# Weight columns for the v and q projections: one cast-on-the-way load per column on GpSimd's queue, or two f32 half loads on SP's queue with a VectorE cast behind each

## Chip, cores and metric

One Trainium2 chip, all 8 NeuronCores; each core runs the same program on its own 2048 tokens. The metric is the device time of the slowest core in microseconds.

## The reference, cut to what matters

A layer on x of shape (2, 8192, 2048): a retention-style attention, a layer norm over x plus its result, then a mixture of 8 experts (top 2) and a second layer norm.

```python
q = (x @ Wq.T).reshape(Bsz, Ls, NHEAD, HEAD_DIM)
v = (x @ Wv.T).reshape(Bsz, Ls, NHEAD, HEAD_DIM)
ret = _retention_scan(v, lam)          # state = lam * state + v_t, along the tokens
out = (q * ret).reshape(Bsz, Ls, D)
out = _layernorm(out, ln_gamma, ln_beta)
g = jax.nn.silu(x @ Wg.T)
out = out * g
return out @ Wo.T
```

and around it `x = _layernorm(x + attn(x))`, `x = _layernorm(x + ffn(x))`, where the feed-forward part is silu(x W1) * (x W3) times the routing weight, then W2, summed over the experts.

## The kernel before

Each core holds 2048 tokens, feature-major (a feature on a partition, tokens along the free dimension), and works on them in two halves of 1024 (`emit_half`, line 486), each in two chunks of 512 columns (CW). A prefix stage first sums the tokens before the core's own, weighted by powers of lambda (lines 357 to 378), so that the scan can start from a carry. All bf16 weights pass through one ring of four SBUF slots, `wring` (line 216), 128 x 2048 bf16 each. `load_wcol` (line 243) takes the next slot and issues a single DMA on GpSimd's queue that reads 1 MB of f32 from HBM and writes it as bf16. It waits only until the matmuls that read the slot four columns ago are done, so the loads run ahead of TensorE.

The stage around the change is the loop over the 16 heads (mt) in lines 517 to 616. Per head:

1. v group: 32 matmuls (16 contraction tiles by 2 chunks, line 525) with a column of Wv into PSUM banks 0 and 1; in half 0 also 16 matmuls of one column (line 537) that apply the same weights to the prefix sum.
2. ScalarE copies v to SBUF (line 552, two copies); VectorE copies the carry (line 561, half 0), scans v along the tokens (line 572) and saves the last state (line 583).
3. q group: 32 matmuls with a column of Wq into banks 2 and 3 (line 596).
4. VectorE multiplies q by the scan's result into yS (line 608, two products).

Every engine runs its instructions in program order. Order between engines is by semaphores alone: each step carries the tokens that it waits for (`Prog.step`, line 56), and a `Buf` collects who last wrote and who read a buffer. A step's place on its engine is the place in this Python code where it is recorded. `begin_write` returns the readers and the last writer that a new write must wait for:

```python
def begin_write(self):
    d = self.readers + ([self.ready] if self.ready else [])
    self.readers = []
    return d
```

Behind the loop come the sums for the layer norm (lines 634, 642), the gate projection (line 663, GpSimd loads again), the norm's rows (`ln_rows_bcast`, line 410) and its application (lines 691 to 705), the output projection (line 737) with its x tiles loaded by SP (line 724), the router, and, behind a barrier, the experts (lines 1012, 1030, 1105) and the last norm with the stores of the output on ScalarE's queue (lines 1194 to 1208). x for a half is loaded as 16 casting DMAs on GpSimd's queue (line 504). The second half's x and first weight columns can be loaded while the first half's tail still runs.

Of the kernel before, what the change touches and what calls it, by code (L numbers as in the profile page):

```python
# [18 lines left out]
F32 = mybir.dt.float32  # L19
# [6 lines left out]
P = 128  # L26
D = 2048
KT = D // P
# [11 lines left out]
class Prog:  # L40

    def __init__(self, nc):
        self.nc = nc
        self.sems = {}
        self.counts = {}
        self.steps = {e: [] for e in ENGINES}
        names = ["dS", "dN", "dX", "pe", "dve", "act", "pool", "sp"]
        names += [f"dG{i}" for i in range(4)] + [f"dR{i}" for i in range(4)]
        names += [f"dW{i}" for i in range(4)] + [f"dA{i}" for i in range(4)]
        names += [f"dC{i}" for i in range(4)]  # L50
        names += [f"out{i}" for i in range(4)]
        for s in names:
            self.sems[s] = nc.alloc_semaphore(s)
            self.counts[s] = 0
# [80 lines left out]
def build(TC=2048, PREF=6144, CW=512):  # L135
# [7 lines left out]
    nc = bass.Bass("TRN2", target_bir_lowering=False)  # L143
    pr = Prog(nc)
# [4 lines left out]
    wq_d = dt("wqT", [KT, P, KT, P], F32, kind="ExternalInput").ap()  # L149
    wv_d = dt("wvT", [KT, P, KT, P], F32, kind="ExternalInput").ap()  # L150
# [65 lines left out]
    wringS = [A(f"wring{i}", [P, KT * P], BF16) for i in range(NWR)]  # L216
# [10 lines left out]
    wring = Ring(NWR)  # L227
# [11 lines left out]
    gbufB = [[Buf() for _ in range(FT)] for _ in range(2)]  # L239
    xcR = Ring(2)  # L240
    ntbR = Ring(2)

    def load_wcol(src_ap):
        s, b = wring.next()
        X = int(np.prod(src_ap.shape[1:]))
        tok = pr.dma("pool",
                     lambda en, t=wringS[s], sr=src_ap, X=X: en.dma_start(  # L247
                         out=t[:, 0:X], in_=sr),
                     deps=b.begin_write(), sem=f"dG{s}")
        b.wrote(tok)  # L250
        return s, b, tok
# [21 lines left out]
        out=wgfS[:], in_=wgf_d.rearrange("p kt e -> p (kt e)")), sem="dX")  # L273
# [5 lines left out]
        out=identf[:], in0=identf[:], scalar1=0.0, scalar2=None,  # L279
# [8 lines left out]
        out=e8f[:], in0=e8f[:], scalar1=0.0, scalar2=None,  # L288
# [6 lines left out]
        out=t16[:], in0=hbetaS[:], scalar1=NEGLN2, scalar2=None,  # L295
        op0=ALU.mult), deps=[t_hbeta])
    t_l0 = pr.tick("act", lambda en: en.activation(
        out=t16[:], in_=t16[:], func=AF.Exp), deps=[t_lpre])
    t_l1 = pr.tick("dve", lambda en: en.tensor_scalar(
        out=lam16[:], in0=t16[:], scalar1=-1.0, scalar2=1.0,  # L300
        op0=ALU.mult, op1=ALU.add), deps=[t_l0])
    t_l2 = pr.tick("dve", lambda en: en.tensor_scalar(
        out=lam16[:], in0=lam16[:], scalar1=1.0, scalar2=TINY,
        op0=ALU.min, op1=ALU.max), deps=[t_l1])
    t_l3 = pr.tick("act", lambda en: en.activation(
        out=loglam16[:], in_=lam16[:], func=AF.Ln), deps=[t_l2])
# [25 lines left out]
    for kt in range(KT):  # L332
        dep = [t_wgf, t_ones_bf]
        if kt == 0:
            dep += psB[5].begin_write()
        wsum_grp = pr.step("pe", lambda en, kt=kt: en.matmul(
            out=psS[5][0:E, 0:1], lhsT=wgfS[:, kt * E:(kt + 1) * E],
            rhs=onescol_bf[:], start=(kt == 0), stop=(kt == KT - 1)),
            deps=dep, inc="pe" if kt == KT - 1 else None)
    psB[5].wrote(wsum_grp)  # L340
    t_wsum = pr.tick("dve", lambda en: en.tensor_copy(
        out=wsumC[:], in_=psS[5][0:E, 0:1]), deps=[wsum_grp])
# [3 lines left out]
    for h in range(NH):  # L346
        t = pr.tick("act", lambda en, h=h: en.activation(
            out=preW[:, h:h + (PT - 1) * NH + 1:NH], in_=cexpS[:],
            func=AF.Exp, scale=loglamP[:, h:h + 1]),
            deps=[t_cexp, t_loglamP])  # L350
        t_preW.append(t)
    t_preWb = pr.tick("dve", lambda en: en.tensor_copy(
        out=preWb[:], in_=preW[:]), deps=t_preW)
# [3 lines left out]
    for j in range(PT):  # L357
        slot, wb, tld = load_wcol(xpre_d[j * P:(j + 1) * P, :])
        last = None
        for c in range(ZCH):  # L360
            dep = [tld, t_preWb]
            if j == 0:
                dep += psB[c].begin_write()
            tok = pr.step("pe", lambda en, j=j, c=c, slot=slot: en.matmul(  # L364
                out=psS[c][0:NH, 0:512],
# [3 lines left out]
                deps=dep, inc="pe" if c == ZCH - 1 else None)  # L369
# [10 lines left out]
    for c in range(ZCH):  # L380
        t = pr.tick("dve", lambda en, c=c: en.tensor_copy(
            out=ZS[:, c * 512:(c + 1) * 512], in_=psS[c][0:NH, 0:512]),
            deps=[z_tok[ZCH - 1]])
# [3 lines left out]
    for kt in range(KT):  # L387
        d4 = psB[4].begin_write()
        tt_ = pr.tick("pe", lambda en, kt=kt: en.transpose(
            out=psS[4][:, 0:NH], in_=ZS[0:NH, kt * P:(kt + 1) * P],  # L390
            identity=identf[0:NH, 0:NH]),
            deps=t_Z + [t_id] + d4)
        psB[4].wrote(tt_)
        te = pr.tick("dve", lambda en, kt=kt: en.tensor_copy(
            out=ZTf[:, kt * NH:(kt + 1) * NH], in_=psS[4][:, 0:NH]),
            deps=[tt_])
# [3 lines left out]
        out=ZTb[:], in_=ZTf[:]), deps=t_ZT)  # L400
# [85 lines left out]
    def emit_half(half, state_prev_half):  # L486
# [3 lines left out]
        with (  # L490
# [5 lines left out]
            nc.sbuf_tensor(f"cbS{half}", [P, 2 * CW], BF16) as cbS,  # L496
            nc.sbuf_tensor(f"ntmpS{half}", [P, 2 * CW], F32) as ntmpS,
            nc.sbuf_tensor(f"x1tS{half}", [P, 3 * CW], F32) as x1tS,
        ):
            xqS = xnS  # L500

            xn_dep = xn_b.begin_write()
            for kt in range(KT):
                t = pr.dma("pool", lambda en, kt=kt: en.dma_start(
                    out=xqS[:, kt * TH:(kt + 1) * TH],
                    in_=xfm_d[kt * P:(kt + 1) * P, hoff:hoff + TH]),
                    deps=xn_dep, sem="dX")
# [7 lines left out]
            state_save = [None] * NH  # L515

            for mt in range(NH):
                slot, wb, tld = load_wcol(wv_d[mt].rearrange("p kt m -> p (kt m)"))
                grp = None
                for kt in range(KT):  # L520
                    for c in range(NCW):
                        dep = [tld, t_xq[kt]]
                        if kt == 0:
                            dep += psB[c].begin_write()
                        grp = pr.step("pe", lambda en, kt=kt, c=c, slot=slot: en.matmul(  # L525
                            out=psS[c][:, 0:CW],
# [3 lines left out]
                            deps=dep,  # L530
                            inc="pe" if (kt == KT - 1 and c == NCW - 1 and half != 0) else None)
                if half == 0:
                    for kt in range(KT):
                        dep = [tld, t_ZTb]
                        if kt == 0:
                            dep += psB[4].begin_write()
                        grp = pr.step("pe", lambda en, kt=kt, mt=mt, slot=slot: en.matmul(
                            out=psS[4][:, mt:mt + 1],
# [3 lines left out]
                            deps=dep,  # L542
# [8 lines left out]
                for c in range(NCW):  # L551
                    ev = pr.tick("act", lambda en, vslot=vslot, c=c: en.copy(  # L552
                        out=vS[:, vslot * TH + c * CW:vslot * TH + (c + 1) * CW],
                        in_=psS[c][:, 0:CW]),
                        deps=[grp] + vdep)
# [30 lines left out]
                    deps=[scan_done[mt]] + sdd)  # L586
                stateB[mt].wrote(state_save[mt])
                rbuf.read(state_save[mt])
                slot, wb, tld = load_wcol(wq_d[mt].rearrange("p kt m -> p (kt m)"))
                grp = None  # L590
                for kt in range(KT):
                    for c in range(NCW):
# [387 lines left out]
        with (  # L980
# [234 lines left out]
            for k in range(4):  # L1215
                tokk = (f"out{k}", pr.counts[f"out{k}"])
                for b in x1R.bufs:
                    b.read(tokk)
        return state_next_half

    st_half = [None] * NH
    for half in range(2):
        st_half = emit_half(half, st_half)

    dma_sems = ["dS", "dN", "dX"] + \
        [f"dG{i}" for i in range(4)] + [f"dR{i}" for i in range(4)] + \
        [f"dW{i}" for i in range(4)] + [f"dA{i}" for i in range(4)] + \
        [f"dC{i}" for i in range(4)] + [f"out{i}" for i in range(4)]
# [89 lines left out]
```

How the kernel before makes its waits and increments, by code:

```python
            def run(engobj):  # L84
                lastwait = {}
                for deps, action, inc, inc_by in self.steps[eng]:
                    for s, v in deps:
                        if lastwait.get(s, 0) < v:
                            engobj.wait_ge(self.sems[s], v)
                            lastwait[s] = v
                    ins = action(engobj)
                    if inc is not None:
                        ins.then_inc(self.sems[inc], inc_by)
```

## Time and profile before

| what | value |
|---|---|
| median of 2 runs | 4673.59 us (4670.37 to 4676.8) |
| profiled execution | 4675.7 us |
| its span on the slowest core (core 1) | 4674.2 us |
| spans of the 8 cores | 4660.2 to 4674.2 us |
| mean granted TensorE clock, core 1 | 0.911 |
| TensorE / VectorE / ScalarE / GpSimd busy | 86% / 23% / 8% / 7% |

Times are microseconds from the start of core 1's span. PE is TensorE, PEld its weight load, DVE VectorE, ACT ScalarE, POOL GpSimd, SP SyncE; a q behind the name is the engine's sequencer, which issues DMAs. L525 is line 525 of the kernel. In a timeline row, a number in brackets is the time that the engine was idle just before, with what ended it. The granted clock is a share of full speed, 2.4 GHz; 0.50 is 1.2 GHz. The sizes of DMAs are those of the bytes written.

### The profile page before, as it was taken

What the parts mean: (1) busy time and instruction counts of PE and PEld (TensorE: products, weight loads), DVE (VectorE), ACT (ScalarE), POOL (GpSimd) and SP (SyncE); (2) the same over time, 40 slices, a digit from 0 to 9 for tenths busy, and PEclk for the clock granted to TensorE, in tenths of its full rate; (3) what the DMA queues carried; (4) which work ended last, traced back from release to release, by engine and by line L of the source; (5) the groups of instructions that cost most, each with busy time, mean ns of one, the idle gap of its engine ahead of it and who ended that gap; (6) DMA issues with size and microseconds to landing.
All of it is one profiled execution on the core that took longest, in us unless ns stands there. A gap on an engine that the chain in (4) does not pass through costs nothing.

```text
span 4674.2 us, 46202 instructions; the slowest of 8 cores (4660.2 to 4674.2 us)
## 1 busy us (share of the span) xinstructions
PE 4000.1 (86%) x17465; PEld 1700.5 (36%) x17465; DVE 1089.9 (23%) x1791; ACT 360.8 (8%) x633; POOL 318.0 (7%) x602
## 2 busy tenths in 40 slices
PE   5699847399999999999959983748999999999994
PEld 1243312144444444444424331213444444444441
DVE  0122061411211211211262206141121121121125
ACT  0002100000000000000020210000000000000001
POOL 2100000000000000000100000000000000000000
PEclk7699968699999999999979995969999999999997
DMA  9853426344654444444454331634465444444442
GB/s 160 134 76 59 64 45 145 92 71 74 125 89 73 68 76 71 68 76 73 69 133 77 62 62 39 142 96 78 75 119 90 70 68 76 72 68 74 75 68 78
DMA packets 136775, 388.98 MB, mean 83 GB/s; under 512 B 15728, under 2 KB 23920, under 8 KB 136560
## 3 DMA queue, kind: packets, MB, share of 16 engines
q0 software_dynamic: 85392, 302.06, 39.8%
q1 hardware_dynamic: 32736, 58.78, 4.2%
q10 hardware_dynamic: 18432, 25.17, 1.6%
q8 instruction: 147, 2.41, 0.2%
q14 instruction: 68, 0.56, 0.0%
HBM read 646.03 MB, written 41.94 MB: 147 GB/s over the span
## 4 chain that ended last, share of the span: by engine, by line
PE 80%; DVE 8%; DMA 5%; issue 4%; ACT 2%; DVEq 0%; POOL 0%; ACTq 0%; POOLq 0%; SPq 0%; PEldq 0%
PE ps L1012 19%; PE ps L1030 19%; PE ps L1105 19%; PE ps L663 5%; PE ps L737 5%; PE ps L525 5%; PE ps L596 5%; DMA wring<-xpre 2%; DVE gbufS L1085 2%; DVE ntmpS L697 1%; DVE ygS L705 1%; DVE ot2S L1194 1%; DVE ntmpS L691 1%; DMA xcS<-x1bhbm 1%; DMA wring<-wvT 1%
## 5 line engine op out<-in xcount | busy, mean ns | idle before, releaser
L1012 PE MATMUL ps<-xnS,wring 128*128 128x512 bf16 x4096 | 925.8, 385 | 109.0 <-DMA wring<-w1T 109.0
L1105 PE MATMUL ps<-gbufS,wring 128*128 128x512 bf16 x4096 | 925.7, 388 | 32.4 <-DVE gbufS L1085 32.4
L1030 PE MATMUL ps<-xnS,wring 128*128 128x512 bf16 x4096 | 904.9, 379 | 0.0
L1012 PEld LDWEIGHTS ps<-xnS,wring 128*128 128x128 bf16 x4096 | 405.1, 99 | 617.5 <-issue 148.6
L1105 PEld LDWEIGHTS ps<-gbufS,wring 128*128 128x128 bf16 x4096 | 405.8, 99 | 556.1 <-issue 96.4
L1030 PEld LDWEIGHTS ps<-xnS,wring 128*128 128x128 bf16 x4096 | 400.7, 98 | 483.4
L1051 DVE TENSOR_TENSOR gbufS<-ps,sh1S 128x512 bf16<-128x512 f32 x256 | 165.0, 686 | 1587.2 <-PE ps L1030 1562.2
L737 PE MATMUL ps<-ygS,wring 128*128 128x512 bf16 x1024 | 269.0, 422 | 120.0 <-DVE ygS L705 120.0
L1045 ACT ACTIVATE sh1S<-ps 128x512 bf16<-128x512 f32 x256 | 139.2, 596 | 2428.9 <-PE ps L1012 2408.6
L525 PE MATMUL ps<-xnS,wring 128*128 128x512 bf16 x1024 | 233.6, 388 | 50.8 <-ACT vS L552 36.2
L663 PE MATMUL ps<-xnS,wring 128*128 128x512 bf16 x1024 | 234.3, 383 | 31.2 <-ACT ygS L676 30.9
L1130 DVE SCALAR_TENSOR_TENSOR x2S<-ps,x2S 128x512 f32<-128x512 f32 x192 | 132.8, 692 | 527.4 <-PE ps L1105 527.4
L596 PE MATMUL ps<-xnS,wring 128*128 128x512 bf16 x1024 | 226.2, 379 | 0.0
L737 PEld LDWEIGHTS ps<-ygS,wring 128*128 128x128 bf16 x1024 | 101.8, 104 | 285.9 <-issue 193.7
L525 PEld LDWEIGHTS ps<-xnS,wring 128*128 128x128 bf16 x1024 | 101.8, 100 | 178.5 <-issue 62.6
L663 PEld LDWEIGHTS ps<-xnS,wring 128*128 128x128 bf16 x1024 | 98.7, 98 | 166.3 <-issue 58.5
L1085 DVE TENSOR_TENSOR gbufS<-ewbS,gbufS 128x512 bf16<-128x512 f32 x256 | 155.4, 687 | 0.0
L247 POOL DMA_DIRECT2D wring<-w1T x128 | 67.6, 528 | 1111.6 <-PE ps L1012 814.3
L596 PEld LDWEIGHTS ps<-xnS,wring 128*128 128x128 bf16 x1024 | 98.9, 98 | 117.1
L364 PE MATMUL ps<-wring,preWb 128*16 128x512 bf16 x192 | 88.4, 615 | 60.3 <-DMA wring<-xpre 57.6
L247 POOL DMA_DIRECT2D wring<-w2T x128 | 67.5, 528 | 926.3 <-PE ps L1105 722.2
L247 POOL DMA_DIRECT2D wring<-w3T x128 | 67.6, 528 | 801.9 <-PE ps L1030 689.2
(135 smaller groups left out, 1380.3 us busy)
## 6 DMA issues: line engine op xcount, KB each, us to landing
wring<-w1T POOLq DMA_DIRECT2D x128, 512.0 KB, 5.1
wring<-w3T POOLq DMA_DIRECT2D x128, 512.0 KB, 5.1
wring<-w2T POOLq DMA_DIRECT2D x128, 512.0 KB, 5.0
wring<-xpre POOLq DMA_DIRECT2D x48, 512.0 KB, 9.7
xf32S<-xfm SPq DMA_DIRECT2D x64, 256.0 KB, 7.6
wring<-wvT POOLq DMA_DIRECT2D x32, 512.0 KB, 5.8
wring<-wqT POOLq DMA_DIRECT2D x32, 512.0 KB, 5.6
wring<-wgT POOLq DMA_DIRECT2D x32, 512.0 KB, 5.4
```

The costliest lines, as they stand in the source:

```text
L247: lambda en, t=wringS[s], sr=src_ap, X=X: en.dma_start(out=t[:, 0:X], in_=sr),
L525: grp = pr.step("pe", lambda en, kt=kt, c=c, slot=slot: en.matmul(out=psS[c][:, 0:CW], lhsT=wringS[slot][:, kt * P:(kt + 1) * P], rhs=xqS[ ...
L596: grp = pr.step("pe", lambda en, kt=kt, c=c, slot=slot: en.matmul(out=psS[2 + c][:, 0:CW], lhsT=wringS[slot][:, kt * P:(kt + 1) * P], rhs= ...
L663: grp = pr.step("pe", lambda en, kt=kt, c=c, slot=slot: en.matmul(out=psS[6 + c][:, 0:CW], lhsT=wringS[slot][:, kt * P:(kt + 1) * P], rhs= ...
L737: grp = pr.step("pe", lambda en, kt=kt, c=c, slot=slot: en.matmul(out=psS[2 + c][:, 0:CW], lhsT=wringS[slot][:, kt * P:(kt + 1) * P], rhs= ...
L1012: g1 = pr.step("pe", lambda en, kt=kt, c=c, slot=slot1: en.matmul(out=psS[c][:, 0:CW], lhsT=wringS[slot][:, kt * P:(kt + 1) * P], rhs=x1nS ...
L1030: g3 = pr.step("pe", lambda en, kt=kt, c=c, slot=slot3: en.matmul(out=psS[2 + c][:, 0:CW], lhsT=wringS[slot][:, kt * P:(kt + 1) * P], rhs= ...
L1045: ts1 = pr.tick("act", lambda en, c=c, shslot=shslot: en.activation(out=sh1S[:, shslot * CW:(shslot + 1) * CW], in_=psS[c][:, 0:CW], func= ...
L1051: tg1 = pr.tick("dve", lambda en, ei=ei, ft=ft, c=c, shslot=shslot: en.tensor_tensor(out=gbufS[:, (ei * FT + ft) * TH + c * CW:(ei * FT + ...
L1085: gd = pr.tick("dve", lambda en, ei=ei, ft=ft, c=c: en.tensor_tensor(out=gbufS[:, (ei * FT + ft) * TH + c * CW:(ei * FT + ft) * TH + (c + ...
L1105: grp = pr.step("pe", lambda en, k=k, c=c, slot=slot2: en.matmul(out=psS[4 + c][:, 0:CW], lhsT=wringS[slot][:, k * P:(k + 1) * P], rhs=gbu ...
L1130: tx2 = pr.tick("dve", lambda en, ht=ht, c=c: en.scalar_tensor_tensor(out=x2S[:, ht * TH + c * CW:ht * TH + (c + 1) * CW], in0=psS[4 + c][ ...
```

## The change

The v and q columns no longer come through `load_wcol`. A new function `load_wcol_sp` takes a slot of the same ring, but loads the column in two halves of 1024 f32 columns (512 KB each) on SP's queue into `wstage`, one staging buffer of 128 x 1024 f32, and records a VectorE copy behind each half that casts it to bf16 into the slot. The second half's load waits for the first half's cast, since there is one staging buffer. A matmul of the group waits for the second cast. The gate, output and expert columns stay on GpSimd's queue. The staging buffer lies in the SBUF that the experts' stage uses for its output tiles, so at the end of a half it takes note of all output stores and of VectorE's and ScalarE's last steps.

```diff
--- before.py
+++ after.py
@@ -44,7 +44,7 @@
         self.sems = {}
         self.counts = {}
         self.steps = {e: [] for e in ENGINES}
-        names = ["dS", "dN", "dX", "pe", "dve", "act", "pool", "sp"]
+        names = ["dS", "dN", "dX", "dF", "pe", "dve", "act", "pool", "sp"]
         names += [f"dG{i}" for i in range(4)] + [f"dR{i}" for i in range(4)]
         names += [f"dW{i}" for i in range(4)] + [f"dA{i}" for i in range(4)]
         names += [f"dC{i}" for i in range(4)]
@@ -239,6 +239,7 @@
     gbufB = [[Buf() for _ in range(FT)] for _ in range(2)]
     xcR = Ring(2)
     ntbR = Ring(2)
+    wstage_b = Buf()
 
     def load_wcol(src_ap):
         s, b = wring.next()
@@ -496,8 +497,27 @@
             nc.sbuf_tensor(f"cbS{half}", [P, 2 * CW], BF16) as cbS,
             nc.sbuf_tensor(f"ntmpS{half}", [P, 2 * CW], F32) as ntmpS,
             nc.sbuf_tensor(f"x1tS{half}", [P, 3 * CW], F32) as x1tS,
+            nc.sbuf_tensor(f"wstage{half}", [P, 1024], F32) as wstage,
         ):
             xqS = xnS
+
+            def load_wcol_sp(src_ap):
+                si, b = wring.next()
+                d = b.begin_write()
+                tld = None
+                HW = (KT * P) // 2
+                for hh in range(2):
+                    tdma = pr.dma("sp", lambda en, src_ap=src_ap, hh=hh, HW=HW: en.dma_start(
+                        out=wstage[:, 0:HW], in_=src_ap[:, hh * HW:(hh + 1) * HW]),
+                        deps=wstage_b.begin_write() + (d if hh == 0 else []),
+                        sem="dF")
+                    wstage_b.wrote(tdma)
+                    tld = pr.tick("dve", lambda en, si=si, hh=hh, HW=HW: en.tensor_copy(
+                        out=wringS[si][:, hh * HW:(hh + 1) * HW],
+                        in_=wstage[:, 0:HW]), deps=[tdma])
+                    wstage_b.read(tld)
+                b.wrote(tld)
+                return si, b, tld
 
             xn_dep = xn_b.begin_write()
             for kt in range(KT):
@@ -515,7 +535,7 @@
             state_save = [None] * NH
 
             for mt in range(NH):
-                slot, wb, tld = load_wcol(wv_d[mt].rearrange("p kt m -> p (kt m)"))
+                slot, wb, tld = load_wcol_sp(wv_d[mt].rearrange("p kt m -> p (kt m)"))
                 grp = None
                 for kt in range(KT):
                     for c in range(NCW):
@@ -586,7 +606,7 @@
                     deps=[scan_done[mt]] + sdd)
                 stateB[mt].wrote(state_save[mt])
                 rbuf.read(state_save[mt])
-                slot, wb, tld = load_wcol(wq_d[mt].rearrange("p kt m -> p (kt m)"))
+                slot, wb, tld = load_wcol_sp(wq_d[mt].rearrange("p kt m -> p (kt m)"))
                 grp = None
                 for kt in range(KT):
                     for c in range(NCW):
@@ -1216,13 +1236,16 @@
                 tokk = (f"out{k}", pr.counts[f"out{k}"])
                 for b in x1R.bufs:
                     b.read(tokk)
+                wstage_b.read(tokk)
+            wstage_b.read(("dve", pr.counts["dve"]))
+            wstage_b.read(("act", pr.counts["act"]))
         return state_next_half
 
     st_half = [None] * NH
     for half in range(2):
         st_half = emit_half(half, st_half)
 
-    dma_sems = ["dS", "dN", "dX"] + \
+    dma_sems = ["dS", "dN", "dX", "dF"] + \
         [f"dG{i}" for i in range(4)] + [f"dR{i}" for i in range(4)] + \
         [f"dW{i}" for i in range(4)] + [f"dA{i}" for i in range(4)] + \
         [f"dC{i}" for i in range(4)] + [f"out{i}" for i in range(4)]
```

VectorE's program from the end of the prefix stage to the first two heads of half 0. Before (ZTb is the prefix sum as bf16; carryS, retS, stateS and yS are the results of the head's steps):

```order
L399 CAST ZTb<-ZTf 128x256 [waits dve]
L561 COPY carryS<-ps 128x1 [waits pe]
L572 SCALAR_TENSOR_TENSOR retS<-lamP,carryS,vS 128x1024 [waits act,dve]
L583 COPY stateS<-retS 128x1 [waits dve]
L608 TENSOR_TENSOR yS<-ps,retS 128x512 [waits pe]
L608 TENSOR_TENSOR yS<-ps,retS 128x512
L561 COPY carryS<-ps 128x1 [waits pe]
```

The same place in the changed kernel:

```order
L400 CAST ZTb<-ZTf 128x256 [waits dve]
L515 CAST wring<-wstage 128x1024 [waits dF] x2
L581 COPY carryS<-ps 128x1 [waits pe]
L592 SCALAR_TENSOR_TENSOR retS<-lamP,carryS,vS 128x1024 [waits act,dve]
L603 COPY stateS<-retS 128x1 [waits dve]
L515 CAST wring<-wstage 128x1024 [waits dF] x2
L628 TENSOR_TENSOR yS<-ps,retS 128x512 [waits pe]
L628 TENSOR_TENSOR yS<-ps,retS 128x512
L515 CAST wring<-wstage 128x1024 [waits dF] x2
L581 COPY carryS<-ps 128x1 [waits pe]
```

Two casts have come in at three places: ahead of the first head, between the state copy and the yS products (q's column of the same head), and behind the yS products (v's column of the next).

SP's program at the change of halves in the changed kernel (x1hbm is the first norm's input kept in HBM, dF the staging loads' semaphore, out0 to out3 those of the output stores):

```order
L1137 DMA xf32S<-x1hbm 128x512 [waits dve,dR0]
L510 DMA wstage<-wvT 128x1024 [waits out0,out1,out2,out3,dve,act,pe,dG0]
L510 DMA wstage<-wvT 128x1024 [waits dve,dF]
L510 DMA wstage<-wqT 128x1024 [waits dve,dF,pe,dG1]
L510 DMA wstage<-wqT 128x1024 [waits dve,dF]
```

SP issued none of these four before; GpSimd's queue held one load for each column, with no wait for the output stores. The first staging load of half 1 waits for all of them.

## Rows read from the trace of the kernel before

**Rows 1.** The page: busy time by engine, and the chain that ended last.
```profile
PE 4000.1 (86%) x17465; PEld 1700.5 (36%) x17465; DVE 1089.9 (23%) x1791; ACT 360.8 (8%) x633; POOL 318.0 (7%) x602
...
PE 80%; DVE 8%; DMA 5%; issue 4%; ACT 2%; DVEq 0%; POOL 0%; ACTq 0%; POOLq 0%; SPq 0%; PEldq 0%
```

**Rows 2.** Window: PE, PEld, DVE, ACT, POOL busy; granted clock, DMA share, GB/s.
```profile
200.00:400.00 200.00, 200.00 (x1127) 93.64 (x1125) 55.32 (x70) 15.06 (x28) 14.77 (x28) 1.00 0.50 74
```

**Rows 3.** Timeline, one q group of half 0: start, length (us), engine, line, tile, count [idle].
```profile
216.04 0.55 PE L537 MATMUL ps<-ZTb,wring 128*128 128x1 bf16 x16
...
216.45 7.07 PE L596 MATMUL ps<-xnS,wring 128*128 128x512 bf16 x32
216.68 1.08 ACT L552 COPY vS<-ps 128x512 f32<-128x512 f32 x2 [13.14 <-PE ps L537]
...
217.93 2.35 DVE L572 TENSOR_TENSOR_SCAN retS<-lamP,carryS,vS 128x1024 f32<-128x1024 f32 x1 [1.07 <-ACT vS L552]
220.38 0.15 DVE L583 COPY stateS<-retS 128x1 f32<-128x1 f32 x1
...
223.35 2.97 PE L525 MATMUL ps<-xnS,wring 128*128 128x512 bf16 x13
223.62 1.29 DVE L608 TENSOR_TENSOR yS<-ps,retS 128x512 bf16<-128x512 f32 x2 [3.09 <-PE ps L596]
```

**Rows 4.** Timeline, the start of the v and q stage in half 0.
```profile
178.59 0.29 DVE L399 CAST ZTb<-ZTf 128x256 bf16<-128x256 f32 x1 [0.96 <-DVE ZTf L394]
...
192.01 9.97 PE L525 MATMUL ps<-xnS,wring 128*128 128x512 bf16 x32 [14.66 <-DMA wring<-wvT]
```

**Rows 5.** DMA answer, 200 to 400 us: a queue's load, issues, median us to landing.
```profile
q0 software_dynamic: 4026, 14.68, 49.8%
...
wring<-wqT POOLq DMA_DIRECT2D x14, 512.0 KB, 5.7
```

**Rows 6.** Timeline, change of halves.
```profile
2393.12 8.54 PE L525 MATMUL ps<-xnS,wring 128*128 128x512 bf16 x32
...
2395.46 48.34 ACTq L1208 DMA_DIRECT2D outfm<-ot2S  x32
...
2444.73 10.02 PE L525 MATMUL ps<-xnS,wring 128*128 128x512 bf16 x32 [36.16 <-ACT vS L552]
```

**Rows 7.** Groups of instructions: VectorE casts, mean ns of one behind the comma.
```profile
L766 DVE CAST cbS<-x1tS 128x512 bf16<-128x512 f32 x64 | 27.4, 427 | 11.1 <-DVE x1tS L750 10.7
...
L352 DVE CAST preWb<-preW 128x768 bf16<-128x768 f32 x1 | 0.6, 559 | 1.8 <-ACT preW L347 1.8
```

**Rows 8.** DMA answer, 885 to 915 us; below it, a load's timeline.
```profile
q1 hardware_dynamic: 1869, 3.41, 39.1%
...
xcS<-x1bhbm SPq DMA_DIRECT2D x14, 256.0 KB, 3.0
...
885.48 4.80 SPq L948 DMA_DIRECT2D xcS<-x1bhbm  x3
...
888.54 0.43 DVE L955 TENSOR_TENSOR ntbS<-xcS,muBb 128x512 bf16<-128x512 bf16 x1 [0.94 <-DMA xcS<-x1bhbm]
```

**Rows 9.** Timeline, TensorE: groups of 32 matmuls after waits of different length.
```profile
453.27 8.92 PE L663 MATMUL ps<-xnS,wring 128*128 128x512 bf16 x32 [2.23 <-ACT ygS L676]
463.14 7.23 PE L663 MATMUL ps<-xnS,wring 128*128 128x512 bf16 x32 [0.94 <-ACT ygS L676]
...
933.30 9.68 PE L1012 MATMUL ps<-xnS,wring 128*128 128x512 bf16 x32 [56.10 <-DMA wring<-w1T]
...
3161.15 8.52 PE L1012 MATMUL ps<-xnS,wring 128*128 128x512 bf16 x32 [52.90 <-DMA wring<-w1T]
```

**Rows 10.** Timeline, TensorE: first matmul behind the last q group, halves 0, 1.
```profile
422.48 0.38 PE L634 MATMUL ps<-yS,onescol_bf 128*1 128x512 bf16 x1
...
2654.97 0.38 PE L634 MATMUL ps<-yS,onescol_bf 128*1 128x512 bf16 x1
```

**Rows 11.** DMA answer, 2406 to 2446 us: the output stores.
```profile
outfm<-ot2S ACTq DMA_DIRECT2D x24, 256.0 KB, 2.2
```

## The prediction

> **What bounds the kernel now.** I read the page first, then stretches of the timeline. TensorE is busy 86% of the span and VectorE 23% [rows 1]; the chain that ended last runs 80% over TensorE. In the stage that the change touches (the projections v and q, once per half) the window of 200 to 400 us in half 0 shows it alone at work: busy 200.00 of 200 us at a granted clock of 1.00, with 55 us of VectorE work beside it [rows 2]. A q group of 32 matmuls takes 6.90 us from its start to that of the next v group (216.45 to 223.35), and in half 0 sixteen small carry matmuls stand behind each v group, 0.4 us [rows 3]. No weight load is on that path: GpSimd issues each up to four columns ahead, and it lands in 5.7 us [rows 5]. So before the change this stage holds no wait that the change could remove, apart from one: 14.66 us ahead of the first v group, which waited for a weight column queued behind the 16 loads of x [rows 4].
>
> **What the change does to the order.** A column's load now has four steps in a row: SP loads 512 KB of f32 into the one staging buffer, VectorE casts it into half of the ring slot, SP may then load the second 512 KB, VectorE casts again. Only the first load can run ahead. The casts stand in VectorE's program order where the loop has the load: q's behind the scan and the state copy of the same head, v's behind the two yS products of the head before. VectorE runs in order, so both casts wait for the group that TensorE has just finished, and TensorE's next group waits for both. The ring of four slots prefetches nothing any more.
>
> **Price of the parts.**
> Cast of 128x1024 f32 to bf16: none stands in the trace. 128x512 took 427 ns and 128x768 559 ns [rows 7]: 132 ns for 256 columns, so 0.69 us.
>
> Load of 512 KB of f32 through SP's queue: none stands there either. From below: 256 KB through the same queue, alone, landed in 3.0 us [rows 8]. From above: the whole column, 1 MB read and cast on the way, 5.7 us [rows 5]. Between them: the 13 or so loads of 256 KB (3.41 MB) in 30 us held the DMA engines 39.1%, 0.9 us each, so 2.1 us of the 3.0 are fixed; doubling the bytes gives 2.1+1.8 = 3.9 us. The casting loads agree: 28 (14 of v's columns and 14 of q's) in 200 us at 49.8% are 3.56 us each, half of it 1.78, and 5.7-3.56 = 2.1 fixed. I take 3.9.
>
> That both halves pay the fixed part is also what the Trainium skill says ("DMA: Bandwidth & Descriptors", section on the anatomy of one DMA, GpSimd path): about 2.0 us plus bytes over 436 GB/s. That is an estimate of 3.2 us for 512 KB and of 2.6 for 256 KB, where the row has 3.0; by it the sum below would be 64 x 0.7 = 45 us lower, some 5330. The row stands higher, so it decides.
>
> Stall from v to q, from [rows 3] (v's last matmul ends at 216.59): ScalarE's two copies begin at 216.68 and end at 217.76, the scan runs from 217.93 to 220.28, the state copy ends at 220.53. Then first cast 0.69, hand-over to SP 0.14 (hand-overs took 0.09 and 0.17 in these rows), load 3.9, hand-over 0.05 (issued at 885.48, landed 3.0 later, used at 888.54 [rows 8]), second cast 0.69, hand-over to TensorE 0.15: 5.62 us, end at 226.15. Stall 9.56 us. The first 512 KB were issued before the v group began and have landed.
>
> Stall from q to v: q ends at 223.52, the two products run from 223.62 to 224.91, 1.39 us; plus 5.62: 7.0 us.
>
> Clock. Now TensorE never stops in this stage and keeps the level of 2.4 GHz (1.00). Where it had idled it restarted on 1.2 GHz: the first groups after 14.66, 36.16, 56.10 and 52.90 us of idleness took 9.97, 10.02, 9.68 and 8.52 us, and after only 2.23 us one took 8.92, against 7.23 for the next, with 0.94 us ahead of it [rows 4, 6, 9]. Every group of the changed stage has 7.0 or 9.6 us of idleness ahead; I take the mean of the four, 9.55 us. This is the clock gate of the Trainium skill ("TensorE: Matmul & The Clock Gate", "What's actually happening": throttled is the default, activity releases it), and the rows agree.
>
> **The sum**, by the timeline of core 1.
> Half 0. The start: the first cast comes behind ZTb's (ends about 178.9 [rows 4]); then 0.69+0.14+the second load+0.69. The DMA engines have 10.7 us less to do there (four columns at 3.56 go, two halves at 1.8 come), but the x loads are still in flight, so I put the start at 187 instead of 192.01. From there 32 groups x 9.55 = 305.6, 16 x 0.4 = 6.4, 16 x 9.56 = 153.0, 15 x 7.0 = 105.0: q of the last head ends at 757. Before it ended at about 422.6, where the sums for the norm begin [rows 10]. Added: 334 us.
> Half 1. Before, v and q of its first head were computed inside half 0's tail (v from 2393.12, q right behind), while VectorE made the last outputs, and v of the second began at 2444.73 [rows 6]. Now the first staging load waits for all outputs: the last is issued at 2443.8 (2395.46+48.34), lands 2.2 us later [rows 6, 11], then load, cast, load, cast: 0.15+3.9+0.05+0.69+0.14+3.9+0.05+0.69+0.15, start at 2455.7. The same 305.6+153.0+105.0 brings its last q to 3019; before it ended at 2655.1 [rows 10]. Added: 364 us, of which some 45 are the lost overlap with the tail.
> Later stages keep their order: GpSimd still prefetches the gate columns, and SP's x tiles for the output projection, now queued behind 64 staging loads (128 loads over both halves), are needed only behind the whole gate stage of 16 groups. Costed at nothing; that stage covers them, and without it each would cost its own load time once.
> Total 4675.7 (the profiled execution; span 4674.2) + 698 = 5374. That execution lies 2 us above the median shown, so about 5372 on its scale; I say 5372.
> A measurement of this kernel can tell about 2% from no change, 93 us.
>
> **Rivals.**
> Clock stays at 1.2 GHz in the whole group: twice the 6.90 us of a full-speed group [rows 3], 13.8 us, so +4.25 x 64 = 272: 5644. For it: idleness in half of the time. Against: each of the four groups after a long wait was under 10.1 us and so came back to 2.4 GHz on its way [rows 4, 6, 9].
> Clock never falls: -2.3 x 64 = -147: 5225. For it: the waits here, 7.0 and 9.6 us, are shorter than the four on which the 9.55 rests. Against: even 2.23 us of idleness were followed by a slow group [rows 9].
> Load as slow as the whole column, 5.7 us: +1.8 x 64 = 115: 5487. For it: eight cores read at once. Against: nothing else of a core is under way.
> Load of 3.0 us and restarts of 8.5: -0.9 x 64 - 1.05 x 64 = -125: 5247.
> The other side: the staged path is hidden. Cast, load and cast are 5.6 us, less than a group of 6.91; if VectorE ran q's casts while v's group runs, no stall would arise, and with the earlier start, -5 us, the time would be 4669, faster by nothing that can be told and not slower. It decides as soon as q's casts stand ahead of the scan and v's ahead of the yS products; the order has all but the first column's behind them. That VectorE is busy only 23% of the span [rows 1] speaks for it, the order against it.
>
> **Chances.** Forecast 0.78; clock low throughout 0.04; clock never falls 0.05; slow load 0.08; both prices low 0.04; hidden 0.01. Range: from 5275 (load 3.4, restarts 8.5: -32 -67) to 5485 (the slow load); what lies outside are parts of the rivals. Only the hidden case is not slower by over 2%: faster 0.005, same 0.005, slower 0.99.
>
> **What would show it.** The v and q groups each idle ahead, 9.6 us with the releaser VectorE (the cast) and 7.0 us; TensorE's busy share over the stage about 55%; granted clock there 0.6 to 0.8; casts of 0.69 us; staging loads landing in 3.9; the stage 570 us long in half 0 instead of 231; TensorE idle through the whole tail of half 0. Wrong it would be if the casts took much longer, if gaps were under 4 us, or if the groups kept 7.2 us.

## The result and the profile after

The changed kernel is slower: 1.144 times the kernel before (95% interval 1.142 to 1.146), which is 5347 us on the scale of the 4673.6 shown. Ratios here rest on undisturbed executions; the median of all 11 runs, 5431.74 us, includes runs in which one die's cores had a lower clock and were slower, as they occur with the kernel before too. The profiled execution took 5351.9 us, its slowest core, core 4, 5350.2; core 1, from which the rows of before come, took 5346.3. The forecast was 5372, its range 5275 to 5485.

The page after, engine totals and the chain that ended last, against [rows 1]:

```profile
PE 4149.5 (78%) x17465; PEld 1734.0 (32%) x17465; DVE 1174.1 (22%) x1919; ACT 360.4 (7%) x633; POOL 284.1 (5%) x538
...
PE 73%; DVE 11%; DMA 8%; issue 4%; ACT 3%; DVEq 0%; POOL 0%; ACTq 0%; SPq 0%; POOLq 0%; PEldq 0%
```

TensorE's matmuls are the same 17465, but its busy share is down from 86% to 78%. In the chain VectorE has risen from 8% to 11% and DMA from 5% to 8%: what TensorE lost was handed to the load and cast steps. Busy time itself rose by 149 us for the same matmuls, 142 of them in the v and q groups (L616 and L545 below); that this is the clock, the fourth experiment shows.

The same window of the v and q stage as in [rows 2]:

```profile
200.00:400.00 200.00, 107.94 (x461) 44.31 (x459) 38.69 (x53) 6.44 (x12) 0.00 (x0) 0.73 0.18 58
```

TensorE is busy 107.94 of 200 us instead of 200.00, at a granted clock of 0.73 instead of 1.00; the DMA engines are busy 18% instead of 50%. Nothing is saturated; everything waits in turn. One head and a half in order of time (core 4, half 0; start, length, engine, line, [idle before, releaser]) shows the turns:

```profile
403.84 0.69 DVE L515 CAST wring<-wstage 128x1024 bf16<-128x1024 f32 x1 [3.72 <-DMA wstage<-wvT]
404.71 15.26 SPq L510 DMA_DIRECT2D wstage<-wqT  x2
...
404.90 9.54 PE L545 MATMUL ps<-xnS,wring 128*128 128x512 bf16 x32 [6.77 <-DVE wring L515]
...
414.28 0.55 PE L557 MATMUL ps<-ZTb,wring 128*128 128x1 bf16 x16
...
415.02 1.07 ACT L572 COPY vS<-ps 128x512 f32<-128x512 f32 x2 [33.54 <-PE ps L557]
416.27 2.35 DVE L592 TENSOR_TENSOR_SCAN retS<-lamP,carryS,vS 128x1024 f32<-128x1024 f32 x1 [1.18 <-ACT vS L572]
418.72 0.15 DVE L603 COPY stateS<-retS 128x1 f32<-128x1 f32 x1
418.83 0.69 DVE L515 CAST wring<-wstage 128x1024 bf16<-128x1024 f32 x1
423.74 0.69 DVE L515 CAST wring<-wstage 128x1024 bf16<-128x1024 f32 x1 [4.22 <-DMA wstage<-wqT]
...
424.69 9.88 PE L616 MATMUL ps<-xnS,wring 128*128 128x512 bf16 x32 [9.87 <-DVE wring L515]
...
434.68 1.29 DVE L628 TENSOR_TENSOR yS<-ps,retS 128x512 bf16<-128x512 f32 x2 [10.24 <-PE ps L616]
435.88 0.68 DVE L515 CAST wring<-wstage 128x1024 bf16<-128x1024 f32 x1
439.93 0.69 DVE L515 CAST wring<-wstage 128x1024 bf16<-128x1024 f32 x1 [3.37 <-DMA wstage<-wvT]
...
440.99 4.25 PE L545 MATMUL ps<-xnS,wring 128*128 128x512 bf16 x12 [6.42 <-DVE wring L515]
```

To be read against [rows 3]. v's group starts at 404.90, its last carry matmul ends at 414.83. ScalarE's copies, the scan and the state copy follow, and only then the first cast of q's column, at 418.83, although its 512 KB were requested at 404.71. The second 512 KB are used at 423.74, 4.22 us after the first cast ended, and q's group starts at 424.69: 9.87 us of idleness. From q to v there are two products, cast, load, cast: 6.42 us.

The groups of instructions, from the page, and the staging loads:

```profile
L616 PE MATMUL ps<-xnS,wring 128*128 128x512 bf16 x1024 | 301.7, 467 | 301.4 <-DVE wring L515 301.4
L545 PE MATMUL ps<-xnS,wring 128*128 128x512 bf16 x1024 | 300.4, 466 | 280.6 <-DVE wring L515 267.1
...
L515 DVE CAST wring<-wstage 128x1024 bf16<-128x1024 f32 x128 | 88.5, 691 | 260.0 <-DMA wstage<-wvT 137.4
...
wstage<-wvT SPq DMA_DIRECT2D x64, 512.0 KB, 3.5
```

Every wait of L616 (q) and all but the first of L545 (v) end with VectorE's cast at L515: 301.4 us over 32 groups, 9.42 each, and 267.1 over 31, of which 57.3 stand ahead of half 1's first group and 7.0 ahead of each other one. The same two groups on the page of before:

```profile
L525 PE MATMUL ps<-xnS,wring 128*128 128x512 bf16 x1024 | 233.6, 388 | 50.8 <-ACT vS L552 36.2
...
L596 PE MATMUL ps<-xnS,wring 128*128 128x512 bf16 x1024 | 226.2, 379 | 0.0
```

There was nothing ahead of q and 50.8 us ahead of v, and the matmuls' mean was 388 and 379 ns, now 466 and 467. The cast takes 691 ns. VectorE is idle for 260.0 us ahead of the casts; all but 6.35 us of it (a first half at the start of half 1) are waits for second halves.

The change of halves, on core 1, against [rows 6]:

```profile
2723.42 43.74 ACTq L1228 DMA_DIRECT2D outfm<-ot2S  x32
...
2769.87 4.81 SPq L510 DMA_DIRECT2D wstage<-wvT  x2
2773.52 0.69 DVE L515 CAST wring<-wstage 128x1024 bf16<-128x1024 f32 x1 [6.78 <-DMA wstage<-wvT]
2778.41 0.69 DVE L515 CAST wring<-wstage 128x1024 bf16<-128x1024 f32 x1 [4.19 <-DMA wstage<-wvT]
...
2779.35 9.91 PE L545 MATMUL ps<-xnS,wring 128*128 128x512 bf16 x32 [58.20 <-DVE wring L515]
```

The last output store is issued at 2767.16 (2723.42+43.74). The first staging load of half 1 goes out at 2769.87 and v's first group starts at 2779.35, 12.2 us behind the last store's issue. Before, two groups had been done by then, and the third began 0.9 us behind it.

Where core 1's time went, from the starts of the marks in both traces (first v group, first sum matmul behind q, first output store, first sum matmul behind q in half 1):

```profile
193.06 9.41 PE L545 MATMUL ps<-xnS,wring 128*128 128x512 bf16 x32 [13.66 <-DMA xnS<-xfm]
...
755.29 0.38 PE L654 MATMUL ps<-yS,onescol_bf 128*1 128x512 bf16 x1
...
3322.99 0.38 PE L654 MATMUL ps<-yS,onescol_bf 128*1 128x512 bf16 x1
```

| stretch, core 1 | before us | after us | difference |
|---|---|---|---|
| start to first v group | 192.0 | 193.1 | +1 |
| v and q stage, half 0 | 230.5 | 562.2 | +332 |
| to the first output store of half 0 | 1973.0 | 1968.1 | -5 |
| from there to the end of half 1's v and q stage | 259.5 | 599.6 | +340 |
| rest | 2019.2 | 2023.3 | +4 |

The 672 us lie where the columns are loaded the new way; the -5 and +4 of the other stretches cancel.

### The profile page after: what moved, and what is told of

Read it like the earlier page. It is cut to its first block, busy times and chain, and to the rows that moved or that the text cites. A ratio compares the mean times of both kernels' runs of the same rounds, so it can differ in the third digit from the quotient of the medians.

```text
span 5350.2 us, 46648 instructions; the slowest of 8 cores (5319.4 to 5350.2 us)
## 1 busy us (share of the span) xinstructions
PE 4149.5 (78%) x17465; PEld 1734.0 (32%) x17465; DVE 1174.1 (22%) x1919; ACT 360.4 (7%) x633; POOL 284.1 (5%) x538
## 4 chain that ended last, share of the span: by engine, by line
PE 73%; DVE 11%; DMA 8%; issue 4%; ACT 3%; DVEq 0%; POOL 0%; ACTq 0%; SPq 0%; POOLq 0%; PEldq 0%
PE ps L1032 17%; PE ps L1050 17%; PE ps L1125 16%; PE ps L616 6%; PE ps L545 6%; PE ps L757 4%; PE ps L683 4%; DMA wstage<-wvT 2%; DMA wstage<-wqT 2%; DMA wring<-xpre 2%; DVE wring L515 2%; DVE retS L592 1%; DVE gbufS L1105 1%; DVE ntmpS L717 1%; DVE ygS L725 1%
## 5 line engine op out<-in xcount | busy, mean ns | idle before, releaser
L1032 PE MATMUL ps<-xnS,wring 128*128 128x512 bf16 x4096 | 927.4, 386 | 102.7 <-DMA wring<-w1T 102.7
L1050 PE MATMUL ps<-xnS,wring 128*128 128x512 bf16 x4096 | 904.9, 379 | 0.0
L1032 PEld LDWEIGHTS ps<-xnS,wring 128*128 128x128 bf16 x4096 | 405.7, 99 | 612.2 <-issue 144.5
L1050 PEld LDWEIGHTS ps<-xnS,wring 128*128 128x128 bf16 x4096 | 400.7, 98 | 483.4
L616 PE MATMUL ps<-xnS,wring 128*128 128x512 bf16 x1024 | 301.7, 467 | 301.4 <-DVE wring L515 301.4
L545 PE MATMUL ps<-xnS,wring 128*128 128x512 bf16 x1024 | 300.4, 466 | 280.6 <-DVE wring L515 267.1
L616 PEld LDWEIGHTS ps<-xnS,wring 128*128 128x128 bf16 x1024 | 115.9, 115 | 480.8 <-issue 416.5
L545 PEld LDWEIGHTS ps<-xnS,wring 128*128 128x128 bf16 x1024 | 117.6, 115 | 464.1 <-issue 399.1
L683 PE MATMUL ps<-xnS,wring 128*128 128x512 bf16 x1024 | 230.8, 379 | 31.2 <-ACT ygS L696 31.0
L683 PEld LDWEIGHTS ps<-xnS,wring 128*128 128x128 bf16 x1024 | 97.6, 97 | 164.0 <-issue 54.0
L515 DVE CAST wring<-wstage 128x1024 bf16<-128x1024 f32 x128 | 88.5, 691 | 260.0 <-DMA wstage<-wvT 137.4
L572 ACT COPY vS<-ps 128x512 f32<-128x512 f32 x64 | 34.4, 589 | 1285.3 <-PE ps L557 701.7
```

The costliest lines, as they stand in the source:

```text
L515: tld = pr.tick("dve", lambda en, si=si, hh=hh, HW=HW: en.tensor_copy(out=wringS[si][:, hh * HW:(hh + 1) * HW], in_=wstage[:, 0:HW]), deps ...
L1032: g1 = pr.step("pe", lambda en, kt=kt, c=c, slot=slot1: en.matmul(out=psS[c][:, 0:CW], lhsT=wringS[slot][:, kt * P:(kt + 1) * P], rhs=x1nS ...
L1050: g3 = pr.step("pe", lambda en, kt=kt, c=c, slot=slot3: en.matmul(out=psS[2 + c][:, 0:CW], lhsT=wringS[slot][:, kt * P:(kt + 1) * P], rhs= ...
```

## The experiments

Theory: the stall ahead of a group is the row of VectorE steps in front of the casts plus cast, second load, cast, and the groups are long because TensorE restarts at 1.2 GHz. Each ratio below is to the kernel before on the same chip; the changed kernel has 1.144.

**Two staging buffers.**

```diff
-    vR = Ring(3)
+    vR = Ring(2)
...
-    wstage_b = Buf()
+    wstage_b = [Buf(), Buf()]
...
-            nc.sbuf_tensor(f"vS{half}", [P, 3 * TH], F32) as vS,
+            nc.sbuf_tensor(f"vS{half}", [P, 2 * TH], F32) as vS,
...
-            nc.sbuf_tensor(f"wstage{half}", [P, 1024], F32) as wstage,
+            nc.sbuf_tensor(f"wstage{half}", [P, 2048], F32) as wstage,
...
-                        deps=wstage_b.begin_write() + (d if hh == 0 else []),
-                        sem="dF")
+                        deps=wstage_b[hh].begin_write() + (d if hh == 0 else []),
+                        sem=["dF", "dE"][hh])
```

The load and the cast of half `hh` use its own 1024 columns of `wstage`. The edit also takes one of the three buffers of v; the third experiment, which has the same two, shows no wait that comes of it.

> The changed kernel with a staging buffer for each half column (v's f32 ring cut from three to two to make room), order of VectorE as changed. Theory (a group's stall is the steps of VectorE in front of the casts, plus cast, second load, cast): the second load and its hand-overs, about 3.9 us, leave each of 64 stalls, v to q 9.4 -> 5.5 us, q to v 7.0 -> 3.0 us: -250, and the restarts stay near 9.4 us or get shorter: 5095 us, between 4980 and 5110. Rival (the loads on SP's queue are the limit, whatever waits): 5348 unchanged.

Measured: ratio 1.080 (1.078 to 1.082), 5048 us on before's scale, so 299 us are back of the 673. Timeline, half 0, slowest core:

```profile
410.07 1.28 DVE L516 CAST wring<-wstage 128x1024 bf16<-128x1024 f32 x2
...
411.72 8.55 PE L546 MATMUL ps<-xnS,wring 128*128 128x512 bf16 x32 [2.96 <-DVE wring L516]
...
424.66 1.29 DVE L516 CAST wring<-wstage 128x1024 bf16<-128x1024 f32 x2
...
426.21 9.82 PE L617 MATMUL ps<-xnS,wring 128*128 128x512 bf16 x32 [5.56 <-DVE wring L516]
```

Both casts now run back to back (1.28 us), and the stalls are 2.96 us ahead of v (L546) and 5.56 ahead of q (L617), 3.5 and 4.3 less than in the timeline after (on core 1's averages 4.0 each). What is left are VectorE's steps in front and the two casts. The load on SP's queue is not the limit: with the second load out of the stalls 299 us came back, with the same bytes on the same queue. That is 50 us more than the 250 of the stalls, and the group lengths account for it: on core 1 a group took 8.45 us on average instead of 9.20, 48 us over 64 groups. The v groups after 2.96 us took 7.07 us in half 1 (all but the first) and mostly 8.4 to 8.6 in half 0.

**Casts one step earlier, one buffer.** q's column is requested and cast ahead of the head's copies and scan, the next v's ahead of the yS products:

```diff
+            nxt_v = load_wcol_sp(wv_d[0].rearrange("p kt m -> p (kt m)"))
             for mt in range(NH):
-                slot, wb, tld = load_wcol_sp(wv_d[mt].rearrange("p kt m -> p (kt m)"))
+                slot, wb, tld = nxt_v
+                nxt_q = load_wcol_sp(wq_d[mt].rearrange("p kt m -> p (kt m)"))
...
-                slot, wb, tld = load_wcol_sp(wq_d[mt].rearrange("p kt m -> p (kt m)"))
+                slot, wb, tld = nxt_q
+                if mt + 1 < NH:
+                    nxt_v = load_wcol_sp(wv_d[mt + 1].rearrange("p kt m -> p (kt m)"))
```

> The changed kernel with one staging buffer, but each column's casts recorded one step earlier: q's ahead of the head's carry copy and scan, the next v's ahead of the yS products. Theory (order of VectorE makes the stall): what is left is the chain load, cast, load, cast of one buffer, 9.0 us per column against a group of 6.9, so 18 us per head instead of 35, and the lost overlap at the change of halves: 4830 us, between 4780 and 4900. Rival 1 (staging hidden once the order is right, as my prediction's hidden case had it, 5.6 us a column): 4670 to 4700. Rival 2 (the load path itself is the limit): above 5250.

Measured: ratio 1.035 (1.031 to 1.040), 4839 us on before's scale. The same loads in the same order on SP's queue, the same casts and the same buffer, only in another order on VectorE, take 508 us off the changed kernel. The order is the main cause; the first experiment's 299 and these 508 overlap, since either shortens the same stalls. Timeline, half 0:

```profile
401.11 0.69 DVE L515 CAST wring<-wstage 128x1024 bf16<-128x1024 f32 x1 [3.39 <-DMA wstage<-wvT]
...
402.17 7.07 PE L547 MATMUL ps<-xnS,wring 128*128 128x512 bf16 x32 [1.28 <-DVE wring L515]
...
409.35 0.69 DVE L515 CAST wring<-wstage 128x1024 bf16<-128x1024 f32 x1 [3.45 <-DMA wstage<-wqT]
...
410.30 7.07 PE L620 MATMUL ps<-xnS,wring 128*128 128x512 bf16 x32 [0.68 <-DVE carryS L583]
...
414.57 0.69 DVE L515 CAST wring<-wstage 128x1024 bf16<-128x1024 f32 x1 [0.90 <-DMA wstage<-wvT]
419.34 0.69 DVE L515 CAST wring<-wstage 128x1024 bf16<-128x1024 f32 x1 [4.07 <-DMA wstage<-wvT]
...
420.39 8.75 PE L547 MATMUL ps<-xnS,wring 128*128 128x512 bf16 x32 [3.03 <-DVE wring L515]
```

The column's second cast comes at 401.11, 409.35 and 419.34: 8.2 and 10.0 us per column, the chain load, cast, load, cast through one buffer, and TensorE waits 0.68 to 3.03 us for it in this stretch (where the row names carryS, that copy stands right behind the cast). So here staging through one buffer is not hidden behind a group of 6.9 us even with the casts in the right place: my hidden case (5.6 us a column) counted only the second load, as if the first had a buffer to wait in.

**Both**, the two diffs above together.

> Both: a staging buffer for each half and the casts one step earlier. Theory: no stall inside the stage, TensorE at granted clock 1.00 there as before; left is the first group of half 1, which waits for the output stores and two casts instead of running in the tail: +23 us: 4697 us, between 4685 and 4715. Rival (VectorE casts or f32 staging traffic slow the matmuls or the other VectorE work): 4750 or more.

Measured: ratio 1.005 (1.003 to 1.007), 4696 us on before's scale. Windows in the stage, core 1 (busy of PE, PEld, DVE, ACT, POOL; granted clock, DMA share, GB/s):

```profile
200.00:400.00 200.00, 200.00 (x1122) 93.51 (x1121) 90.14 (x124) 15.03 (x28) 0.00 (x0) 1.00 0.42 140
2460.00:2640.00 180.00, 180.00 (x836) 81.61 (x835) 83.73 (x105) 13.98 (x27) 0.00 (x0) 1.00 0.48 152
```

200.00 of 200 and 180.00 of 180 us at clock 1.00, as before the change, with 90 instead of 55 us of VectorE work and with f32 staging traffic beside them. The casts and the traffic cost nothing inside the stage: on core 1 all q and v groups but the first of each half took 7.07 us. The rival of a disturbance by them is out, and so is the choice of SP's queue. What is left of the loss lies outside: on core 1 the stretch from the first output store of half 0 to the end of half 1's v and q stage took 276.9 us against 259.5 before, 17 of the expected 23, and the first v group of all started at 198.50 instead of 192.01, which was not expected: the 19.25 us of idleness ahead of it end with a load of x.

**Matmuls in the gaps.** Nothing is taken away; 39 matmuls behind each v group and 27 behind each q group but the last of a half fill the idle time. Their results are read by nobody:

```diff
+                nfill = 39
+                for r in range(nfill):
+                    dep = psB[5].begin_write() if r == 0 else []
+                    tf = pr.step("pe", lambda en, slot=slot: en.matmul(
+                        out=psS[5][:, 0:CW],
+                        lhsT=wringS[slot][:, 0:P],
+                        rhs=xqS[:, 0:CW], start=True, stop=True),
+                        deps=dep, inc="pe" if r == nfill - 1 else None)
...
```

The same stands behind the q group with `nfill = 27 if mt + 1 < NH else 0`.

> The changed kernel with matmuls whose result nobody reads placed in the idle time: 39 behind each v group (8.4 us), 27 behind each q group but the last of a half (5.8 us), into a free PSUM bank, from the slot just used. Nothing is taken away. Theory (the long groups are restarts at 1.2 GHz): groups go from 9.4 to 7.2 us, -2.2 x 64 = -140: 5208 us, between 5190 and 5250, granted clock near 1.00 in the stage. Rival (groups are long because casts or staging traffic disturb them): 5348 or more, clock unchanged.

Measured: ratio 1.116 (1.113 to 1.118), 5213 us on before's scale: 134 us faster than the changed kernel with 2058 matmuls more. The same kernel, executed once more:

> The kernel with matmuls in the gaps once more, for its trace. Theory: groups of 32 near 7.2 us and granted clock 0.95 or more between 200 and 400 us, ratio 1.115. Rival: groups near 9.4 us and clock 0.73, as in the changed kernel.

Measured: 5222.4 us. The window of 200 to 400 us on core 1, then two windows and parts of the timeline of core 7, the slowest:

```profile
200.00:400.00 200.00, 187.45 (x945) 84.83 (x944) 43.34 (x58) 7.25 (x14) 0.00 (x0) 1.00 0.21 69
...
200.00:400.00 200.00, 197.17 (x869) 84.25 (x868) 39.50 (x54) 6.44 (x12) 0.00 (x0) 0.85 0.19 64
400.00:600.00 200.00, 187.44 (x960) 84.96 (x958) 43.50 (x59) 7.52 (x14) 0.00 (x0) 1.00 0.21 69
...
245.67 8.57 PE L627 MATMUL ps<-xnS,wring 128*128 128x512 bf16 x32
...
402.64 8.58 PE L571 MATMUL ps<-xnS,wring 128*128 128x512 bf16 x39
...
411.24 0.69 DVE L515 CAST wring<-wstage 128x1024 bf16<-128x1024 f32 x1 [3.76 <-DMA wstage<-wqT]
...
412.08 7.07 PE L627 MATMUL ps<-xnS,wring 128*128 128x512 bf16 x32 [0.86 <-DVE wring L515]
...
425.83 7.07 PE L545 MATMUL ps<-xnS,wring 128*128 128x512 bf16 x32 [0.86 <-DVE wring L515]
```

L545 and L627 are the v and q groups, L571 and L640 (behind q) the filling. With about 0.9 us instead of 9.4 or 7.0 ahead of them the groups take 7.07 us, and on core 1 every group of the stage but the first of each half does; the granted clock there is 1.00 from 200 us on, as expected. In the same window the clock of cores 0 to 5 is 1.00. Cores 6 and 7 had a granted clock of 0.81 from 198 to 358 us, and core 7's groups in it took 8.57 or 8.58 us. That is no restart: these groups have no idleness at all ahead of them (the row at 245.67), and the level is neither 1.00 nor 0.50. The loads keep their time (3.76 us of wait ahead of the second cast). So the long groups of the changed kernel, 9.2 us on average, come from the clock after idleness: with the idleness filled they are gone, with loads, casts and order unchanged.

**First two columns of half 1 by GpSimd.**

```diff
-                slot, wb, tld = load_wcol_sp(wv_d[mt].rearrange("p kt m -> p (kt m)"))
+                slot, wb, tld = (load_wcol if half and mt == 0 else load_wcol_sp)(wv_d[mt].rearrange("p kt m -> p (kt m)"))
```

and the same for wq_d.

> The changed kernel, but the first v and the first q column of half 1 come through the old load on GpSimd's queue; all others as changed. Theory: both groups run in half 0's tail again, and the first staged column is the second head's v, which still starts 12 us after the last output store: one pair with its two stalls (9.4+9.4+9.4+7.0) leaves the path: -35 us, ratio to before 1.137 instead of 1.144. Rival (the tail's stores and VectorE work hold these groups up anyway): no change, 1.144.

Measured: ratio 1.130 (1.119 to 1.141), a wide interval that holds 1.137 and not the rival's 1.144. The trace shows where the time went. From the first output store to the end of half 1's stage on core 1: 2708.83 to 3274.00, 565.2 us against 599.6, 34 us less for the expected 35.

```profile
2706.49 8.56 PE L545 MATMUL ps<-xnS,wring 128*128 128x512 bf16 x32
...
2708.83 44.10 ACTq L1228 DMA_DIRECT2D outfm<-ot2S  x32
...
2714.89 7.07 PE L616 MATMUL ps<-xnS,wring 128*128 128x512 bf16 x32
...
2764.14 8.74 PE L545 MATMUL ps<-xnS,wring 128*128 128x512 bf16 x32 [42.18 <-DVE wring L515]
```

Both groups run in the tail (2706.49, 2714.89), and the first staged v group starts 11.2 us behind the last store's issue (2752.93), where the first group of the changed kernel started 12.2 behind it. How exactly 34 meets 35 is in part luck: core 1's whole span is 62 us shorter than in the changed kernel, and 28 of them lie in stretches whose code is the same. The v and q stage of half 0 alone took 552.6 us here and 562.2 there; so two executions of the same code differ by 10 us in this stage.

**The same with both repairs.** The kernel of the third experiment with half 1's first v and q column by GpSimd.

> Two staging buffers, casts one step earlier, and the first v and q column of half 1 by GpSimd. Theory: what the two-buffer early kernel still lost (ratio 1.005) is the pair of groups at the change of halves; with them back in the tail 15 to 17 us return: ratio 1.001, between 0.999 and 1.003. Rival (the 1.005 comes from the 128 casts or from f32 traffic all over the stage): ratio stays 1.004 or more.

Measured: ratio 0.999 (0.994 to 1.004). That is the time of before, but the interval is too wide to tell 1.001 from 1.004, so the ratio does not show the 15 to 17 us. The trace does. Core 1, the first output store of half 0 and the end of half 1's v and q stage:

```profile
2392.09 43.73 ACTq L1233 DMA_DIRECT2D outfm<-ot2S  x32
...
2652.78 0.38 PE L659 MATMUL ps<-yS,onescol_bf 128*1 128x512 bf16 x1
```

That is 260.7 us, against 276.9 with both repairs alone (2396.01 to 2672.88) and 259.5 before: 16 us are back. No version of staging beat the kernel before.

**Two casting loads per column, no staging**, in the kernel before:

```diff
+    def load_wcol_2(src_ap):
+        s, b = wring.next()
+        d = b.begin_write()
+        for hh in range(2):
+            tok = pr.dma("pool",
+                         lambda en, t=wringS[s], sr=src_ap, hh=hh: en.dma_start(
+                             out=t[:, hh * 1024:(hh + 1) * 1024],
+                             in_=sr[:, hh * 1024:(hh + 1) * 1024]),
+                         deps=d, sem=f"dG{s}")
+            d = []
...
```

> The kernel before, with each v and q column loaded by two casting DMAs of half its width on GpSimd's queue, no staging, no cast on VectorE. Theory (a second fixed part costs nothing as long as loads run ahead through the ring): same time, ratio 1.000. Rival (splitting a column is itself what costs): some 2 us per column, 64 x 2 = 128 us, ratio 1.03.

Measured: ratio 0.996 (0.992 to 1.000), no cost. Loading a column in two pieces cost nothing here, where the loads run ahead and nobody waits for the second; in the changed kernel VectorE does.

## Why the prediction was right

Its forecast of 5372 lies 25 us, 0.5%, above what was measured. The mechanism was right; that the number came this close is in part luck, as the terms below show. Step by step:

The order of VectorE was the cause named, and moving the casts alone returned 508 of 673 us.

The cast: 0.69 forecast, 691 ns measured.

The load: 3.9 us forecast from the doubling of a 256 KB load. The median is 3.5 us, for the second halves as for all, and the second halves of core 4 but the first took 3.6 us on average. VectorE's idle time ahead of the casts, 260.0 us, less 9.96 and 6.35 for the first columns of the two halves, is 3.9 us over the other 63 waits, hand-overs included, where 4.1 were forecast. So the forecast was 0.2 to 0.3 us too long. The Trainium skill's fit ("DMA: Bandwidth & Descriptors", the anatomy of one DMA, which is for GpSimd's queue) gives an estimate of 3.2 us; the load on SP's queue lies between the two.

The stalls, on core 1, from its groups of instructions:

```profile
L616 PE MATMUL ps<-xnS,wring 128*128 128x512 bf16 x1024 | 290.2, 453 | 302.9 <-DVE wring L515 302.9
...
L545 PE MATMUL ps<-xnS,wring 128*128 128x512 bf16 x1024 | 298.8, 464 | 279.8 <-DVE wring L515 266.1 <-DMA xnS<-xfm 13.7
```

v to q 9.56 forecast, 9.47 measured (302.9 us over 32); q to v 7.0 forecast, 6.93 measured (266.1 us, less 58.2 ahead of half 1's first group, over 30).

The groups: 9.55 forecast, the mean of four restarts of before. Measured on core 1: 9.26 and 9.35 in half 0 (v, q), 9.41 and 8.79 in half 1, 9.2 in all. 64 x 0.35 = 22 us too much. The term was sized from four samples between 8.5 and 10.0, and it does not stay the same from one execution to the next, as half 0 shows, whose q groups took 9.35 us here and 9.04 in the fifth experiment, with the same code.

The start of half 0: 187 forecast, 193.1 measured, 6 us too little. Two things were missed there: the second staging load took long while the x loads were in flight (9.96 us of wait ahead of its cast on core 4, where the other second halves had 3.9), and the first group then waited for x itself (the 13.66 us of idleness before it end with DMA xnS). Its column was there at 192.5, before x.

The change of halves: start 12.0 us behind the last store's issue forecast, 12.2 measured. Not costed: the tail itself became 4.6 us shorter (43.74 against 48.34 us over its 32 stores). No weight load ran beside the stores any more. The other kernels fit: the tail took 48.96 us with the columns in two casting loads, where such loads run beside the stores, and 43.7 to 44.1 in all that stage the next columns, also with both groups back in the tail (44.10 and 43.73). That the loads are the cause was not tried by itself.

Together, on core 1: the groups 22 us too long, the stalls of half 1 5 and the tail 5, against 6 too little at the start. That makes the 26 us between the 698 forecast and the 672 measured. The late start cancelled part of the rest, so the sum fits better than its terms.

Rivals: the clock low throughout (groups of 13.8 us) and the clock never falling (7.2) both fell by the group lengths of 9.2; a load of 5.7 us fell by the waits of 3.9. The hidden case was wrong in its own price, as the second experiment shows.

## What to carry to other kernels

A cast that an in-order engine does for another's input must be recorded where its data is ready, ahead of the steps that wait for the previous result; one step too late, and an early load is of no use, as the 508 us of the second experiment show. Count the buffers of a staged path by its period: with one buffer for two halves it is twice load plus cast, whatever may be requested early. And idleness of TensorE was paid twice here: the 62 stalls behind the first groups of the halves were 511 us on core 1, and the slow restarts another 134, which came back when the idle time was filled.

## What the runs showed of the hardware

The same gap does not always have the same effect on the clock. In the kernel with two buffers every v group but the first of each half followed about 3 us of idleness (2.96 in nearly all). On core 1, in half 1 all fifteen of them ran at full speed (7.07 us), in half 0 two did and thirteen took 8.4 us or more. The q groups, after 5.5 us, mostly took 8.4 in half 1 and 9.8 in half 0. Nor does a longer gap always cost more: with the casts one step earlier (core 5), v groups after 2.91 and 3.35 us took 7.07, and others after 2.09 and 2.19 took 8.75. In the two-buffer kernel the lengths stay the same for many heads in a row, so it looks as if the rhythm of work and idleness settles in one phase; what decides which was not tried.

A granted clock below 1.00 does not always mean idleness either: in the filled kernel cores 6 and 7 stood at 0.81 for 160 us while core 7 was never idle, and a group of 32 matmuls took 8.57 us.
